# A routed feed-forward kernel: moving the last pair's second layer one step later, and reloading the shared weights' low halves in eight pieces

## The reference, cut to what matters

```
x = x + tanh(g_xattn) * attention(layernorm(x), ctx)          # 2048 tokens of 256
xf = layernorm(x)
shared = (gelu(xf @ sw1[s] + sb1[s]) @ sw2[s]  summed over 2 s  + biases) / 2
gates = xf @ router_w + router_b;  the 2 best of 8 experts, softmax of the two
moe    = sum over the token's 2 experts of  prob * (gelu(xf @ w1[e] + b1[e]) @ w2[e] + b2[e])
out = x + tanh(g_ffn) * (shared + moe)                         # hidden size 512
```

## Time and profile before

| what | value |
|---|---|
| median of 3 runs | 384.3 us (382.98 to 384.43) |
| the profiled execution | 384.16 us |
| its span, first to last instruction | 382.4 us |
| outside the span | 1.76 us |
| PE busy | 372.3 us (97%) |
| PE weight loads / DVE / ACT / POOL busy | 353.1 / 282.1 / 242.0 / 220.1 us |
| granted TensorE clock | 1.000 of full speed |

### The profile page before, as it was taken

How to read it: one execution, slowest core, us unless ns; L and a number is a source line. 1 busy time by engine, 2 the same in 40 slices (tenths; PEclk the granted TensorE clock), 3 DMA queues, 4 the chain that set the end, 5 groups by cost and what they waited for, 6 DMA issues and landing times.

```text
span 382.4 us, 8794 instructions
## 1 busy us (share of the span) xinstructions
PE 372.3 (97%) x2773; PEld 353.1 (92%) x2774; DVE 282.1 (74%) x612; ACT 242.0 (63%) x540; POOL 220.1 (58%) x262
## 2 busy tenths in 40 slices
PE   8999999999999999999999999999999998899996
PEld 7898889999999999999999989999999996779996
DVE  5798799978988988799899886555555653445486
ACT  2777545655664654887869857666666654667850
POOL 8367657688878764477782245566666564543100
PEclk9999999999999999999999999999999999999999
DMA  7990000001000058501950112222232323641397
GB/s 228 312 326 3 2 14 29 16 21 35 14 14 14 29 177 304 236 4 22 270 154 2 27 45 85 71 70 83 83 86 79 98 84 111 195 116 39 99 351 252
DMA packets 33263, 40.15 MB, mean 105 GB/s; under 512 B 9610, under 2 KB 26444, under 8 KB 33100
## 3 DMA queue, kind: packets, MB, share of 16 engines
q1 hardware_dynamic: 28384, 29.40, 24.8%
q0 software_dynamic: 4768, 10.28, 8.8%
q10 hardware_dynamic: 76, 0.02, 0.0%
HBM read 27.88 MB, written 11.68 MB: 103 GB/s over the span
## 4 chain that ended last, share of the span: by engine, by line
PE 85%; DMA 4%; DVE 3%; ACT 3%; issue 3%; POOL 2%; DVEq 0%; ACTq 0%; POOLq 0%
PE psum L1327 12%; PE psum L1350 12%; PE psum L1287 10%; PE psum L1243 9%; PE psum L1589 8%; PE psum L1495 6%; PE psum L1469 5%; PE psum L1550 4%; PE psum L1210 3%; DMA xsl<-y_rows,table 3%; PE psum L1129 2%; PE psum L1167 2%; PE psum L1191 2%; PE psum L1275 1%; PE psum L1482 1%
## 5 line engine op out<-in xcount | busy, mean ns | idle before, releaser
L739 POOL DMA_INDIRECT y_tok<-ysl,table x39 | 39.1, 1002 | 39.6 <-ACT ysl L1025 34.7
L732 POOL DMA_INDIRECT xsl<-y_rows,table x39 | 39.0, 1000 | 37.0 <-PE psum L1458 12.5
L705 POOL DMA_INDIRECT names<-named,pos x32 | 35.5, 1109 | 12.8 <-issue 8.2
L658 POOL TENSOR_TENSOR Eb<-Eb,rinv 128x512 f32<-128x512 f32 x32 | 33.5, 1066 | 13.1 <-DVE rinv L1801 13.1
L1066 ACT ACTIVATE hr<-psum,b_cur 128x256 f32<-128x256 f32 x48 | 20.2, 472 | 22.1 <-DVE b_cur L2094 12.3
L901 ACT ACTIVATE yTb<-psum 128x256 f32<-128x256 f32 x16 | 6.2, 385 | 42.6 <-PE psum L1307 42.6
L1589 PE MATMUL psum<-xsT_hi,w_cur 128*128 128x256 f32 x192 | 30.9, 283 | 0.0
L2138 DVE TENSOR_TENSOR hr_lo<-hr,hr_hi 128x512 fp32r<-128x512 f32 x24 | 16.6, 693 | 14.9 <-ACT hr_hi L1079 14.6
L641 POOL TENSOR_TENSOR half_sum<-Eb 128x512 f32<-128x512 f32 x16 | 20.6, 1288 | 12.1 <-ACT Eb L856 11.9
L1025 ACT ACTIVATE ysl<-psum,table 128x256 f32<-128x256 f32 x39 | 17.0, 467 | 16.1 <-PE psum L1469 11.3
L1589 PEld LDWEIGHTS psum<-xsT_hi,w_cur 128*128 128x128 f32 x192 | 26.5, 192 | 0.0
(11 more groups left out here) (276 smaller groups left out, 1257.5 us busy)
## 6 DMA issues: line engine op xcount, KB each, us to landing
w_raw<-in_L_ffn_w SPq DMA_DIRECT2D x2, 4096.0 KB, 16.8
y_got<-y_tok SPq DMA_DIRECT2D x8, 512.0 KB, 8.1
xs_all<-in_x SPq DMA_DIRECT2D x4, 512.0 KB, 12.0
sw_raw<-in_L_ffn_sw SPq DMA_DIRECT2D x2, 1024.0 KB, 13.8
y_rows<-ybuf SPq DMA_DIRECT2D x16, 128.0 KB, 1.7
sw_lo_kept<-sw_lo SPq DMA_DIRECT2D x1, 2048.0 KB, 6.6
sw_lo<-sw_lo_kept SPq DMA_DIRECT2D x4, 512.0 KB, 4.4
out<-xs_all SPq DMA_DIRECT2D x3, 512.0 KB, 3.1
```

The lines of the kernel that those rows point to most:

```text
L658: nc.gpsimd.tensor_tensor(Eb[q][:, heads, :], Eb[q][:, heads, :], rinv[:, q, heads].unsqueeze(2).broadcast_to([P, H // 2, CTX]), ALU.mult) ...
L705: nc.gpsimd.indirect_dma_start(names, bass.IndirectOffsetOnAxis(ap=pos[:, k, t:t + 1], axis=0), named[:, k, t, :], None).then_inc(scattere ...
L732: nc.gpsimd.indirect_dma_start(into[:, s % 2, :], None, y_rows, bass.IndirectOffsetOnAxis(ap=table[:, s, 0:1].bitcast(I32), axis=0)).then_ ...
L739: nc.gpsimd.indirect_dma_start(y_tok, bass.IndirectOffsetOnAxis(ap=table[:, s, 1:2].bitcast(I32), axis=0), ysl[:, s % 2, :], None).then_in ...
```

## The change

give_wide(28) moves on PE from step(30) to step(31), behind turn(32). On ACT, output(28) and output(29) move with it to step(31), and `turned(31)` moves from step(30) into double(11), ahead of output(26) and output(27). ACT's hr_hi of tile 30 now waits for `half_used`, until give_wide(28) has read the first half. On DVE the bias copy and the hs copy of tile 30 move from step(30) into double(11), between the two hr_lo of the pair. On SP the four loads of 512 KB become eight of 256 KB: the first of two behind each table, the second one when the hsT of a step is done; PE's wait for all of them counts 32 per table in place of 16.

```diff
 SP, behind each of the last four tables (n = 0 to 3)
-                    sp.wait_ge(h_psum, SINGLE1 + n)
-                    piece = slice(n * 2 * SW_WORDS // BACK, (n + 1) * 2 * SW_WORDS // BACK)
-                    sp.dma_start(sw_s[1][:, piece].bitcast(F32), sw_lo_kept[:, piece]).then_inc(sw_moved, 16)
+                    for i in range(2):
+                        if i == 0:
+                            sp.wait_ge(h_psum, SINGLE1 + n)
+                        else:
+                            sp.wait_ge(ht_psum, SINGLE1 + n + 1 - 2 * DOUBLES)
+                        piece = slice((2 * n + i) * SW_WORDS // BACK, (2 * n + i + 1) * SW_WORDS // BACK)
+                        sp.dma_start(sw_s[1][:, piece].bitcast(F32), sw_lo_kept[:, piece]).then_inc(sw_moved, 16)
 ACT, step
                 elif s + 1 < SLOT_TILES:
-                    turned(s + 1, 1 - par)
+                    if s != SINGLE1:
+                        turned(s + 1, 1 - par)
-                if s == SINGLE1:
-                    output(s - 2, 0)
-                    output(s - 1, 1)
-                elif s >= 2 and s != SINGLE1 + 1:
+                if s == SINGLE1 + 1:
+                    output(s - 3, 0)
+                    output(s - 2, 1)
+                elif s >= 2 and s != SINGLE1:
                     output(s - 2, par)
...
                 act.wait_ge(ht_raw, s + 1)
+                if s == SINGLE1:
+                    act.wait_ge(half_used, 2 * DOUBLES)
                 nc.scalar.activation(hr_hi[:, par, :, :], hr[:, :, :], ACT.Copy).then_inc(ht_hi, 1)
 ACT, double
                 kept(1)
+                if d == DOUBLES - 1:
+                    turned(SINGLE1 + 1, 1)
                 output(s - 2, 0)
 PE, step
-                if s == SINGLE1:
-                    give_wide(s - 2, 1)
-                elif s >= 2 and s != SINGLE1 + 1:
+                if s == SINGLE1 + 1:
+                    give_wide(s - 3, 1)
+                elif s >= 2 and s != SINGLE1:
 PE, ahead of the rest of the shared part
-            pe.wait_ge(sw_moved, 16 + 16 * BACK)
+            pe.wait_ge(sw_moved, 16 + 32 * BACK)
 DVE, step and double
-            def step(s, par):
+            def bias_and_hidden(s, par):
                 if s >= 2:
                     dve.wait_ge(ht_raw, s - 1)
                 bias_of(s, par).then_inc(b1_ready, 1)
                 dve.wait_ge(h_psum, s + 1)
                 nc.vector.tensor_copy(hs[:, :], bank[2 + par][:, :]).then_inc(h_ready, 1)
+            def step(s, par):
+                if s != SINGLE1:
+                    bias_and_hidden(s, par)
...
+                if d == DOUBLES - 1:
+                    bias_and_hidden(SINGLE1, 0)
                 half_left(1)
```

## The result

The changed kernel took 380.62 us median (379.86 to 382.36, 7 runs) against 384.01 (382.98 to 384.86, 7 runs) of the kernel before; the ratio is 0.9915, 95% interval 0.9892 to 0.9938. Predicted were 381.0 (380.2 to 383.3). It is faster by 3.4 us.

What follows compares the result with a forecast made beforehand. PE, busy 97% of the span, was taken as the bound, so time is won only where it idles or has less to do. 384.16 - 2.4 + 0.4 - 1.2 = 380.96, so 381.0 us, range 380.2 to 383.3.

Steps and rivals of the forecast that it cites:

- The three waits have one root: PE's waits of 1.23 before give_wide(28), 0.57 before hsT(31) and 1.35 before h(32) were said to share one root.
- term one: PE from h(30) to h(32): the new order brings h(32) earlier, minus 2.4 us, bounds 0.9 and 3.15.
- hs copy hidden: DVE's hs copy of tile 30 hides in 1.63 us of DVE idle; h(31) begins at 319.36.
- The new wait is hidden by 0.05: ACT's hr_hi(30) waits for half of give_wide(28); turned(32) allows h(32) at 324.25, PE itself only at 324.3.
- Rival B: hr_hi(30) on ACT is released near give_wide(28)'s end, about 1.5 later; 382.1 us, chance 0.09.
- term two: PE's turn(34) in step(33): gather(34) lands 0.2 late, with part of a restart plus 0.4 us, bounds 0 and 1.5.
- term three: PE's turn(36): with eight smaller loads gather(36) lands in time, minus 1.2 us, bounds 0 and minus 1.2.
- Rival C: Smaller loads make the DMA engines dearer, gathers 34, 36 and 37 take 6.8 each; slower, 386.6 us, chance 0.04.
- Rival D: The move only shifts PE's idle to the next gathers; 383 to 384.2 us, chance 0.15.

Runs made afterwards that it cites:

- e5: Changed kernel with sw_lo back in the four 512 KB loads (order only, repeat); 395.37 us, ratio 0.9928 to the kernel before.
- e7: Changed kernel with give_wide(28) back in step(30) on PE (repeat); 397.54 us, ratio 1.0008 to the kernel before.
- e2: Kernel before with the eight 256 KB loads alone; 395.21 us, ratio 0.9974 to the kernel before.
- e6: Kernel before with the eight 256 KB loads alone, repeat; 396.68 us, ratio 0.9967 to the kernel before.
- e4: Changed kernel with DVE's bias and hs copies of tile 30 back in step(30); 397.09 us, ratio 1.0001 to the kernel before.
- e11: Changed kernel with DVE's bias and hs copies of tile 30 back in step(30), repeat; 399.51 us, ratio 0.9987 to the kernel before.
- e1: Changed kernel with sw_lo back in the four 512 KB loads (order only, first run); 396.76 us, ratio 1.0005 to the kernel before.
- e10: Control of after: the changed kernel unedited, under the later conditions; 397.78 us, ratio 0.9964 to the kernel before.
- e12: Changed kernel without SP's wait for hsT between a table's two 256 KB loads; 396.79 us, ratio 0.9991 to the kernel before.
- e3: Changed kernel with give_wide(28) back in step(30) on PE (first run); 397.84 us, ratio 1.0055 to the kernel before.
- e9: Control of before: the kernel before unedited, under the later conditions; 399.88 us against 399.39, ratio 1.003.

## Why the prediction was right, step by step

*The three waits have one root and go with the order (term one, minus 2.4).* Right in place and size: 2.46. e5 shows 2.0 of it without the loads (10.91 to 8.92), e7 that it needs PE's part; that it needs ACT's too is argued. That the waits have one root is not so. I put the 4.20 us of ACT's wait down to the scatter's landing and took 4.48 as given; in e2 and e6 the loads alone take away the wait before h(32), worth 1.1, while the one of 1.2 before give_wide(28) stays. The gains of the two edits overlap in this segment (2.0 and 1.1 alone, 1.84 together in the control), so how much of the 2.46 the order gave cannot be read from the first pair.

*hs copy hidden, h(31) at 3.48 after h(30).* Measured 3.46, hs at 316.87, 1.68 after h(30) as worked out. What the copy's place is worth was not shown (e4, e11).

*The new wait is hidden by 0.05.* In the first trace it was, by some 0.03 (0.18 less the 0.15 that always lies between xsT_lo and its h). In e1, e5, e10 and e12 it was not: PE waited 0.27 to 0.44. Rival B was the right thing to fear, at under half of its price: the first segment of e5, e10 and e12 is 0.53 to 0.68 longer than in the first trace, where B had 1.5.

*gather(34) late by 0.2, with the restart 0.4 (term two).* The term that was mis-sized: it cost nothing. The gather was issued at 325.15 and landed after 2.8, where I had 3.75 as the middle of my bounds; its due time was 328.54. The load ahead of it had been issued at 323.9 and landed after 2.9, the next one went out at 326.3, so it lay mostly between two loads; that this is why it was fast is argued, not shown. The term was no mistake in kind: in e3, behind two loads 0.5 apart, the same gather made PE wait 0.82, and there h(33) to h(34) took 1.21 more, which is within the bounds I had (0 to 1.5).

*gather(36) in time with eight loads (term three, minus 1.2).* Right in size for the profiled pair: 1.19, with 5.0 to landing against a slack of 5.24 (issued at 330.26, due at 335.50; I had 5.3). So it was in time by 0.24 only. As a mechanism it is shown only in part. With four loads PE waited before turn(36) in two traces of four (0.89 in the first, 0.33 in e5; none in e1, e9), with eight in none of ten, of which three, the first trace, e2 and e6, had neither a hold nor a late gather(34) that could have given it time. That fits, but four traces are few: what the loads take away is a wait that comes in some executions, not 1.2 us in each.

*Rival C, dearer small loads.* Not seen. In the first two traces each load of 256 KB landed after 2.9 to 4.2, each of 512 KB after 4.1 to 6.4; the later traces give no landing times. The Trainium skill ("DMA: Bandwidth & Descriptors", section "Anatomy of one DMA — SWDGE (gpsimd) path") gives about 2.0 us fixed for each DMA issued from GpSimd; the prediction named another section of the page for it and left out that these loads are issued from SyncE. Their two medians here, 3.1 and 4.4, leave by my estimate 1.8 for a load of no bytes, so they do not speak against the figure, though no run isolates it. The advice of the same page of the Trainium skill (section "Measured (HBM→SBUF, 128 partitions, SWDGE, issued from GpSimd)"), at least 1 MiB a transfer, is given for bandwidth. Here the loads had time to spare (the last was in at 335.0, the stage that needs them began at 349.3) and the gathers beside them had not; going from 512 to 256 KB paid, and no run tried 1 MiB.

*Rival D, the idle only shifts.* It did not in the first runs. In the later ones it did in part: to DVE's hold in step(33), which is not a gather, and in e3 to gather(34).

Of the sum, only term two was off by more than 0.1. Without it the sum is 380.6, the measured median; that the two agree to 0.1 is in part chance, since single executions lie between 379.86 and 382.36. The profiled execution took 379.93, lower by the 0.7 won ahead of h(30), which no term forecast.

## What to carry to other kernels

When one engine's output waits for a DMA to land, look at what stands behind it in that engine's order before you shorten the DMA; then look at what transfers run beside the DMA too, since here either edit alone removed a good part of the same stall. Try the smaller edit by itself first: the loads alone took 30.7 us where the whole change took 31.6. A background reload with time to spare is worth cutting up and spreading out, so that a gather or scatter on which an engine waits has few bytes beside it. A wait that is hidden by less than 0.2 us in one trace should be counted as exposed. When an edit is taken apart, compare each part with a kernel that has the same other parts, or one edit's gain is booked to another.

## What the runs showed of the hardware that was not expected

PE idle time can cost more than its length: after PE had been busy 0.58 us out of 2, the granted clock was 0.53 and 0.61 over the next 4 us, and a step took 5.05 us in place of 3.48 (e9). In e3 PE was busy 0.19 us of 2, and then the clock was 0.52 and 0.63. The waits of e9 in another execution, the first trace of before, with PE busy 0.65 us of 2, left the clock at 1.00.

A whole condition of 14 us more (398 against 384) came with holds of 1 to 4.6 us on DVE, ACT and POOL, for which the trace names no releaser, one of them at the same instruction in nearly each kernel of one order. The first two traces have no such hold. What it is was not settled. The edit, worth 3.4 us before, gave medians 1.6 apart there (397.78 against 399.39), and a ratio that cannot be told from 1.
